# Four quarters instead of three of the experts' up weights in fp32r products

## What is computed

```python
he = jnp.einsum('nd,edh->enh', xf, expert_w1) + expert_b1[:, None, :]     # 512 -> 768, gate and up interleaved
te = swiglu5(he, ...)        # clip both, g * sigmoid(g * alpha) * scale * (u + shift): 384 left
oe = jnp.einsum('enh,ehd->end', te, expert_w2) + expert_b2[:, None, :]    # 384 -> 512
y = jnp.einsum('ne,end->nd', cw, oe)                                      # cw: weights of the two chosen
```

## Time and profile before

| | |
|---|---|
| time, median of 3 runs (lowest to highest) | 863.76 us (862.98 to 864.32) |
| the profiled execution: time, span of its core | 863.68 us, 861.7 us |
| mean granted clock of PE in it | 0.967 |
| busy: PE, VectorE, ScalarE, GpSimd | 792.2 (92%), 528.1 (61%), 321.1 (37%), 139.2 us (16%) |
| chain that ended last: PE, VectorE, issue, ScalarE | 77%, 15%, 4%, 2% of the span |
| L1378, busy in all, three groups of 168 | 73.2 + 57.3 + 56.9 us |
| L1425, L1372, busy in all | 78.6 us, 45.5 us |
| L2006 (VectorE), L976 (ScalarE), busy in all | 74.0 us, 64.2 us |
| the experts' blocks | from about 620 us to the end |

### The profile page before, as it was taken

The page is one execution under the profiler, slowest core; times in us unless marked ns, Lnnn a source line. Parts: engine busy times, 40 slices in busy tenths (PEclk is TensorE's granted clock), DMA queues, the critical chain, the costliest instruction groups (busy, mean ns, idle before and its releaser), DMA issues.

```text
span 861.7 us, 13555 instructions
## 1 busy us (share of the span) xinstructions
PE 792.2 (92%) x3933; PEld 618.9 (72%) x3934; DVE 528.1 (61%) x943; ACT 321.1 (37%) x542; POOL 139.2 (16%) x186
## 2 busy tenths in 40 slices
PE   3899899999999989997999969988989999999983
PEld 1556788888888876676888857877867777777761
DVE  7787832421441487887023675897487878778751
ACT  1563512521431204533211253332255555556531
POOL 2000000000000210000000500212134343545321
PEclk9999899999999998998999998987999999999997
DMA  7500000000000010000101103002998949874632
GB/s 173 162 1 2 1 1 1 1 0 1 1 1 1 31 52 0 1 1 1 49 1 45 72 2 120 1 0 90 335 339 271 312 94 361 268 201 73 155 60 35
DMA packets 32292, 71.39 MB, mean 83 GB/s; under 512 B 4387, under 2 KB 4637, under 8 KB 32243
## 3 DMA queue, kind: packets, MB, share of 16 engines
q1 hardware_dynamic: 24480, 53.31, 17.8%
q0 software_dynamic: 6272, 14.68, 8.5%
q10 hardware_dynamic: 1491, 2.73, 0.9%
HBM read 96.53 MB, written 12.72 MB: 127 GB/s over the span
## 4 chain that ended last, share of the span: by engine, by line
PE 77%; DVE 15%; issue 4%; ACT 2%; DMA 1%; DVEq 1%; ACTq 0%; POOL 0%; POOLq 0%
PE PS L1125 22%; PE PS L1159 10%; PE PS L1378 9%; PE PS L1425 8%; PE PS L1257 5%; PE PS L1067 4%; PE PS L1372 4%; PE PS L1200 3%; PE PS L1410 3%; PE PS L1049 2%; PE PS L1356 1%; PE PS L1387 1%; PE PS L1098 1%; DVE XN L1495 1%; PE PS L1302 1%
## 5 line engine op out<-in xcount | busy, mean ns | idle before, releaser
L1125 PE MATMUL PS<-CTR,YH 125*128 125x500 f32 (+1 forms) x480 | 164.4, 358 | 2.3 <-DVE YL L1683 2.3
L1125 PE MATMUL PS<-CTR,YL 125*128 125x500 f32 (+1 forms) x480 | 163.8, 356 | 0.0
L1125 PEld LDWEIGHTS PS<-CTR,YH 125*128 125x128 f32 x480 | 91.6, 191 | 15.6 <-DVE YL L1683 2.6
L1125 PEld LDWEIGHTS PS<-CTR,YL 125*128 125x128 f32 x480 | 91.8, 191 | 13.0
L2006 DVE TENSOR_TENSOR W1L<-WB,W1H 128x1152 fp32r<-128x1152 f32 x56 | 74.0, 1356 | 17.1 <-issue 10.1
L1425 PE MATMUL PS<-WB,YF 128*128 x168 | 78.6, 605 | 2.5 <-issue 1.7
L1710 DVE TENSOR_TENSOR ZL<-PS,ZH 128x500 fp32r<-128x500 f32 (+1 forms) x36 | 21.1, 591 | 90.4 <-ACT ZH L789 90.4
L1378 PE MATMUL PS<-W1H,XGH 128*128 128x384 f32 x168 | 73.2, 436 | 0.0
L976 ACT CAST W1H<-WB 128x1152 fp32r x56 | 64.2, 1151 | 16.3 <-issue 11.0
L1378 PE MATMUL PS<-W1L,XGH 128*128 128x384 f32 x168 | 57.3, 341 | 0.0
L1378 PE MATMUL PS<-W1H,XGL 128*128 128x384 f32 x168 | 56.9, 339 | 0.0
(11 more groups left out here) (393 smaller groups left out, 1638.9 us busy)
## 6 DMA issues: line engine op xcount, KB each, us to landing
WB<-in_w SPq DMA_DIRECT2D x28, 1536.0 KB
WB<-in_w SPq DMA_DIRECT2D x28, 768.0 KB
WB<-in_b SPq DMA_DIRECT2D x28, 384.0 KB
X<-in_x SPq DMA_DIRECT2D x1, 2240.0 KB
xn_dram<-XN SPq DMA_DIRECT2D x1, 2240.0 KB
WNEXT<-in_W SPq DMA_DIRECT2D x2, 1024.0 KB, 10.1
SR<-in_sw SPq DMA_DIRECT2D x1, 1536.0 KB, 7.7
out<-X ACTq DMA_DIRECT2D x1, 1120.0 KB
```

Of the source, the lines that this page charges most:

```text
L1125: mm = nc.tensor.matmul(dest, lhs, rhs, start=(t == 0 and h == 0), stop=(t == NT - 1 and h == 1))
```

## The change

`FR` becomes `FT`, so all four quarters of w1 and of the turned rows are rounded, split, and multiplied with three fp32r products. The fp32 product, its copy `xgf`, its semaphore `xgt_f` and PE's value load for it go. The casts and subtractions of w1 grow from [128, 3, 384] to [128, 4, 384], those of the rows from 384 to 512 elements. The buffers grow by a third; `W1H1` now covers tiles 0 to 5 of X, and `HEAD` becomes 6 for that reason.

```diff
--- before.py
+++ after.py
@@ -93,8 +93,8 @@
 ASSIGN = TOPK * NT
 LENT = (1, 3, 5, 7)
 AHEAD = 5
-HEAD = 5
-FR = 3
+HEAD = 6
+FR = FT
 WIDE = ((0, 112), (112, NP))
 
 
@@ -307,7 +307,7 @@
         w1_in = [sem("w1_in0"), sem("w1_in1")]
         w2_in = [sem("w2_in0"), sem("w2_in1")]
         xt_ps, xgt_ready = sem("xt_ps"), sem("xgt_ready")
-        xgt_hi, xgt_f, w1_hi, w1_lo, out_head = sem("xgt_hi"), sem("xgt_f"), sem("w1_hi"), sem("w1_lo"), sem("out_head")
+        xgt_hi, w1_hi, w1_lo, out_head = sem("xgt_hi"), sem("w1_hi"), sem("w1_lo"), sem("out_head")
         hb_ready, clip_done, clip_g, gate_sig, t_gs, t_ready = (
             sem("hb_ready"), sem("clip_done"), sem("clip_g"), sem("gate_sig"), sem("t_gs"), sem("t_ready"))
         clip_u = sem("clip_u")
@@ -363,7 +363,6 @@
         W1L = [at("W1L0", R_YL + ROWB - W1B, [128, FR, H2], F32R), at("W1L1", R_X + W1B, [128, FR, H2], F32R)]
         XGH = at("XGH", R_YH + 4096, [128, 2, FR, 128], F32R)
         XGL = at("XGL", R_YL + 4096, [128, 2, FR, 128], F32R)
-        xgf = YF[:, 1792:2048].rearrange("p (b n) -> p b n", b=2)
 
         rat = [2 * INTER]
 
@@ -962,7 +961,6 @@
 
             def rows_hi(k, b):
                 act.wait_ge(xt_ps, b + 1)
-                nc.scalar.copy(xgf[:, k, :], PS[:, 4, FR * 128:D]).then_inc(xgt_f, 1)
                 nc.scalar.copy(XGH[:, k, :, :], PS[:, 4, 0:FR * 128].rearrange("p (f n) -> p f n", f=FR)
                                ).then_inc(xgt_hi, 1)
 
@@ -1351,7 +1349,6 @@
                 pe.wait_ge(gathered[k], i * 16 + 16)
                 if not (isinstance(b, int) and b < 1):
                     pe.wait_ge(xgt_ready, b)
-                    pe.wait_ge(xgt_f, b)
                 for f in range(FT):
                     mm = nc.tensor.transpose(PS[:, 4, f * 128:(f + 1) * 128], xg[:, k, f * 128:(f + 1) * 128], ident[:, :])
                 mm.then_inc(xt_ps, 1)
@@ -1361,22 +1358,18 @@
                     pe.wait_ge(clip_done, p - 1)
 
             def up(k, b, between):
-                off = pe.value_load(eb_i[0:1, 1, bass.ds(b, 1)], min_val=0, max_val=(NWB - 1) * WBUF)
-                pe.wait_ge(xgt_f, b + 1)
                 up_bank_free(b)
                 for h in range(2):
                     if h and between:
                         between()
                     cols = slice(h * INTER, (h + 1) * INTER)
                     pe.wait_ge(w1_lo, b * 2 + (h + 1))
-                    nc.tensor.matmul(PS[:, 2 * k + h, 0:INTER], xgf[:, k, :],
-                                     WB[:, bass.ds(off + (FR * H2 + h * INTER), INTER)], start=True, stop=False)
                     if h == 0:
                         pe.wait_ge(xgt_ready, b + 1)
                     for f in range(FR):
                         for j, (x, wt) in enumerate(((XGH, W1H), (XGL, W1H), (XGH, W1L))):
                             mm = nc.tensor.matmul(PS[:, 2 * k + h, 0:INTER], x[:, k, f, :], wt[k][:, f, cols],
-                                                  start=False, stop=(f == FR - 1 and j == 2))
+                                                  start=(f == 0 and j == 0), stop=(f == FR - 1 and j == 2))
                 mm.then_inc(hb_ready, 1)
 
             def turn_act(k, p):
```

## The result

The changed kernel takes **875.21 us** (median of 4 runs, 875.14 to 876.12), the kernel before 863.87 (4 runs, 862.98 to 864.32): a ratio of **1.0142**, 95% interval 1.0122 to 1.0162. The forecast was 875.4. The profiled execution of the changed kernel took 876.12 us, with a span of 874.1, 12.4 us more than before.

A forecast was written before the change was run, and what follows sets the result against it. PE bounds the kernel before; afterwards the serial round through VectorE, ScalarE and VectorE's queue does. Terms 0.8 + 1.0 + 8.1 + 0.3 + 0.5 + 1.0 = +11.7 us on about 863.7 give 875.4 us, range 866.5 to 882.0.

The forecast's parts named there:

- PE is the bound before and would need 7.53 us after: Experts' blocks: PE sets the pace at 7.78 us a block; fewer passes would cut its need by 0.25 us.
- Sizes of casts and subtractions: ScalarE's casts of w1 grow to 1.47 us (+0.32 each), VectorE's subtractions to 1.75 us (+0.40 each), two per block.
- about 7.3 us in a block: VectorE's busy time in an expert block after the change, up some 0.9 us, still below PE's 7.53.
- First kind of block +0.26: Block of a pair without the way round the loop: next L2020 at +7.96 us instead of +7.70.
- Second kind +0.55: Block of a pair with the way round the loop: next L2020 at +8.41 us instead of 7.86.
- the queue's 2.39 us: VectorE's queue, from second cast's end round the loop to next L2020: 0.65 us, two value loads of 0.75, and 0.24.
- Loop 8.1: Ten full pairs of blocks in the loop, each 16.37 us instead of 15.56, add 8.1 us.
- stray loads 1.0: Queue loads that take far longer, no longer hidden by slack, add 1.0 us in all; bounds 0 and 3.
- Start 0.8: Before the first block: last store still releases VectorE, two longer subtractions delay L2020 by 0.8 us; bounds 0 and 1.2.
- Four blocks ahead of the loop 1.0: Four written-out blocks, each slower by 0.26 us like the first kind, add 1.0 us; bounds 0 and 2.
- Last block, exit: One block of the first kind adds 0.3 us; leaving the loop later, less a shorter last half, adds 0.5.
- the rival of the falling clock: Experts' blocks: PE's new idle time throttles its clock in a quarter of each block, +30 us, 905 us; chance 0.04.

The follow-up runs named there:

- E8: Changed kernel with first cast ahead of the sigmoid, result behind the second cast, expert's number loaded later, slot's place loaded once: 868.38 us, ratio 1.0047.
- E1: Changed kernel's twelve fp32r products per half, but ScalarE casts and VectorE subtracts only three quarters of w1: 861.12 us, ratio 0.9956.
- E5: Changed kernel with the load of the expert's number moved behind L2013 in VectorE's queue: 866.82 us, ratio 1.0042.
- E10: Kernel before with `HEAD` = 6 and nothing else: 864.36 us, ratio 0.9999.
- E2: Kernel before, fp32 product kept, with casts and subtractions of four quarters (fourth unused) and `HEAD` = 6: 876.59 us, ratio 1.0107.
- E12: Changed kernel with GpSimd copying a scatter's row numbers ahead of the wait for the scatter before: 875.55 us, ratio 1.0141.
- E4: Changed kernel, but ScalarE casts three quarters while VectorE subtracts four, `WB` from itself: 866.98 us, ratio 1.0032.
- E7: Changed kernel with the expert's number loaded behind L2013 and ScalarE's result behind the second cast: 872.02 us, ratio 1.0084.
- E11: E8 with GpSimd copying a scatter's row numbers ahead of the wait for the scatter before: 862.09 us, ratio 0.9985.

## Why the prediction was right, point by point

- **PE is the bound before and would need 7.53 us after.** Right: E8's 7.51, and E1's gain.
- **Sizes of casts and subtractions.** Right to 0.01 us. The sum for VectorE's busy time, "about 7.3 us in a block", should have given 7.2 (145.71 us of 182.00 in blocks of 7.78, plus 0.93); 156.88 us in blocks of 8.3 are 7.15. The forecast doesn't use it.
- **First kind of block +0.26.** Right as the shortest form: 7.94 to 7.97 in 5 of the 11 blocks of this kind in the loop, 8.03 to 8.50 in the others. In the block at 726.39 ScalarE's steps lie within 0.01 us of their forecast, VectorE's first subtraction 0.04 before it.
- **Second kind +0.55, by the queue's 2.39 us.** Right: 2.43 in the chain, blocks of 8.41 to 8.60 in the loop, half of them 8.41 to 8.44; E5 shows it by taking one load off the round. The 0.30 us of a value load stands in both traces; the 600 ns that the Trainium skill (DMA: Bandwidth & Descriptors, Latency and other measured facts) puts as the floor of a `tensor_load` would have given, as the prediction estimated, about 890 us, which the result excludes.
- **Loop 8.1, stray loads 1.0.** The 20 blocks took 155.6 us before and 166.1 after, +10.5. Ten pairs of the short form, 7.95 + 8.43, make +8.2. The other 2.3 us are the blocks that took longer: the stray load at 711.39 belongs to one of 8.50. So the stray loads and the like were mis-sized, 1.0 for 2.3, within the bounds given. That all of the 2.3 is stray loads is not shown.
- **Start 0.8.** Mis-sized. From the last L2031 (L2038) at 618.15 (620.12) to the first L2013 (L2020) at 626.42 (628.31) are 8.27 us, 8.19 before: +0.1. The last store was not last any more: block 1's first subtraction, which waited 4.95 us for it, now waits for ScalarE's cast and starts at 623.08, 0.7 us earlier by that count. VectorE in order of time, changed kernel:

```profile
623.08 3.43 DVE L1999 TENSOR_TENSOR W1L<-WB,W1H 128x1536 fp32r<-128x1536 f32 x2 [4.23 <-ACT W1H L974]
...
635.38 0.96 DVE L2013 TENSOR_TENSOR bias<-PS,WB 128x768 f32<-128x768 f32 x1 [1.36 <-PE PS L1371]
```

- **Four blocks ahead of the loop 1.0.** Mis-sized: 30.4 us before, 33.4 after, +3.0, outside the bound of 2. The first of them, 8.96 for 7.00, has two thirds of it. The prediction sized it by the round of VectorE and ScalarE, but here the next L2013 waits for PE (1.36 us, the row above), and the sum has nothing for PE at half clock. PE in order of time:

```profile
624.89 0.44 PE L1371 MATMUL PS<-W1H,XGH 128*128 128x384 f32 x1 [2.17 <-DVE W1L L1999]
...
627.18 0.52 PE L1371 MATMUL PS<-W1H,XGL 128*128 128x384 f32 x1
...
630.49 0.90 PE L1380 MATMUL PS<-ident,RT 128*128 128x128 f32 x3 [2.47 <-DVE RT L2026]
...
632.15 0.52 PE L1371 MATMUL PS<-W1H,XGH 128*128 128x384 f32 x1
```

  PE waited 2.17 us, fell to half clock at about 626 us, waited another 2.47, and came back to full clock at about 636.5 (a product takes 0.52 us at half clock and 0.34 at full, one following another after 0.32 and 0.17). The twelve products of this block's second half took 4.0 us from 631.04, against 2.1 for the twelve from 617.95 at full clock, which is in size about what this block lost. The kernel before also fell to half clock here, after a wait of 2.41 us, but its next wait was 1.21 and it was back at full clock ahead of the second half. From 620 to 640 us the granted clock was 0.74; in the kernel before it was 0.91, and with `HEAD` = 6 alone (E10) 0.83. The rows, in this order:

```profile
620.00:640.00 20.00, 15.37 (x63) 12.92 (x62) 14.18 (x17) 10.59 (x12) 3.87 (x5) 0.74 0.87 310
```

```profile
620.00:640.00 20.00, 16.39 (x72) 12.82 (x71) 13.13 (x18) 9.53 (x14) 3.53 (x5) 0.91 0.87 299
```

```profile
620.00:640.00 20.00, 16.44 (x66) 12.56 (x65) 12.08 (x16) 7.97 (x12) 3.25 (x5) 0.83 0.83 290
```

  E10's first block took 8.36 us, so in its trace the longer half clock is there without the longer splits, though its time is not measurably longer. E1, with `HEAD` = 6 and short splits too, had 0.91 and a first block of 8.25, so the clock is not all of it. Start and the four blocks together (last L2038 or L2031 to the fifth L2020 or L2013) took 38.6 us before, 41.7 after, 41.5 in E2, 39.7 in E10 and 37.8 in E1. So most of the +3.1 goes with the longer splits; these are single traces, and how much belongs to `HEAD` stays open.
- **Last block, exit.** +0.24 (forecast 0.3), and exit with the last half +0.4 (0.5). Right.
- **The clock in the loop.** It stayed at 1.00 with PE idle 0.45 us in a block (10 us in 22 blocks; 0.65 was forecast). A wait in every block did not bring the clock down there, and the rival of the falling clock is out. The earlier trace rows spoke less firmly than I took it, though: the same stretch of unchanged code shows a clock of 0.89 in the changed kernel's trace, against 1.00 before.
- **What hid the mis-sized terms.** The changed kernel's profiled execution reached the last L2031 1.97 us before the other reached its L2038, in code that the edit doesn't touch. The terms behind it add up to +14.4 us, 2.7 more than the 11.7 forecast, and the head start took 2.0 of that back. The profiled execution also lies 0.9 us above the median of its kernel. So the median met the forecast to 0.2 us partly by luck; the steps as such carried an error of 1 to 3 us.

The terms: +0.1 start, +3.0 ahead of the loop, +10.5 loop, +0.2 last block, +0.4 exit and last half, +0.2 behind it, less 2.0 for the head start, 12.4 us in all.

## What to carry to other kernels

A table of busy times gives the bound only if no ring of serial waits through several engines is longer than the busiest of them: lay out one period in order of time, and add the queue's loads and branches behind the last wait. Before giving the bounding engine less work at the cost of others, shorten that ring first (here a load moved behind the instruction that doesn't need it), and ask what comes next: here the scatters. A chain of waits names what ended last, not what would move the end; E12 took a named part away and nothing moved.

## What the runs showed of the hardware

- A queue that has stood at a semaphore did its loads only afterwards: 2.4 us from the release to the engine's next instruction round the loop, with two value loads of 0.30 us each, 0.70 with the work around them.
- At the start of the experts' blocks PE fell to half clock after one wait of 2.1 to 2.4 us (kernel before, E10, changed kernel). The wait that followed was 1.21, 1.43 and 2.47 us, and the granted clock from 620 to 640 us 0.91, 0.83 and 0.74. In the loop of the changed kernel, with waits of up to 1.1 us in every block of 8.3 us, the granted clock stayed at 1.00.
- Executions of one program spread over 9 to 13 us in ten runs of versions with a shorter round (E4, E7, E8, E11), against 4 to 7 us in 13 to 25 runs of the kernel before and 1 us in the four of the changed kernel.
- VectorE's clip, 0.48 us as a rule, took 0.55 to 0.60 us in some blocks (735.48, 735.95) and up to 0.78, in both kernels; what it met there was not settled.
